# Regrouping VectorE's four steps of a unit, and TensorE's fills, in a four-layer selective scan

## The reference

```
delta = softplus(dt_proj(x) + bias)
h[t]  = exp(delta[t] * A[d, n]) * h[t-1] + (delta[t] * u[t]) * B[t, n]
y[t]  = sum over n of h[t][n] * C[t, n]  +  D * u[t]
```

## Time and profile before

| what | value |
|---|---|
| median of 3 runs | 36,397.4 us (36,394.3 to 36,398.0) |
| span of the profiled execution | 36,378.3 us |
| VectorE busy | 33,161.5 us, 91% |
| GpSimd busy | 30,847.6 us, 85% |
| TensorE busy | 26,866.7 us, 74% |
| ScalarE busy | 18,959.8 us, 52% |
| mean granted TensorE clock | 0.848 of full |
| multiplies of VectorE (L1051) | 6,240 |
| scans of VectorE in V units, in P units | 6,240 and 3,744 |

### The profile page before, as it was taken

The page is one execution under the profiler, slowest core; times in us unless marked ns, Lnnn a source line. Parts: engine busy times, 40 slices in busy tenths (PEclk is TensorE's granted clock), DMA queues, the critical chain, the costliest instruction groups (busy, mean ns, idle before and its releaser), DMA issues. The chain is left out here.

```text
span 36378.3 us, 340417 instructions
## 1 busy us (share of the span) xinstructions
PE 26866.7 (74%) x79280; PEld 8195.4 (23%) x79280; DVE 33161.5 (91%) x18001; ACT 18959.8 (52%) x23286; POOL 30847.6 (85%) x7804
## 2 busy tenths in 40 slices
PE   5777777777766777777777766777777777766777
PEld 2222222222222222222222222222222222222224
DVE  5999999999977999999999977999999999976993
ACT  4555555555534555555555534555555555534551
POOL 1999999999961999999999951999999999964994
PEclk7888888888888888888888888888888888887886
DMA  4666666666675666666666665666666666675665
GB/s 154 173 172 174 175 173 175 174 173 174 173 221 168 175 172 174 175 174 175 174 174 174 174 216 168 174 174 173 173 175 175 174 174 174 174 218 181 175 174 148
DMA packets 2423694, 6402.41 MB, mean 176 GB/s; under 512 B 703824, under 2 KB 875728, under 8 KB 2411728
## 3 DMA queue, kind: packets, MB, share of 16 engines
q1 hardware_dynamic: 2421968, 6387.69, 65.8%
HBM read 2986.75 MB, written 764.47 MB: 103 GB/s over the span
## 5 line engine op out<-in xcount | busy, mean ns | idle before, releaser
L1277 POOL TENSOR_TENSOR h<-h,c 128x2048 f32<-128x2048 f32 x4992 | 20780.7, 4179 | 660.1 <-DVE h L1077 522.6
L1077 DVE TENSOR_TENSOR_SCAN h<-decay,state,slot 128x1024 f32<-128x1024 f32 x6240 | 14647.7, 2347 | 789.0 <-ACT state L1221 32.3
L906 PE MATMUL slot<-bc,pick 96*128 96x512 bf16 x12496 | 4544.6, 452 | 7554.3 <-DVE h L1073 6883.1
L983 PE MATMUL psy<-h,t_fold 128*32 128x512 f32 x40000 | 9979.5, 671 | 0.0
L1073 DVE TENSOR_TENSOR_SCAN h<-slot,state,made 128x1024 f32<-128x1024 f32 x3744 | 8548.9, 2325 | 6.5 <-ACT slot L1116 5.3
L1298 POOL TENSOR_TENSOR made<-du,b 128x2048 f32<-128x2048 f32 x1872 | 7811.8, 4173 | 683.0 <-DMA b<-bcdram 683.0
L1116 ACT ACTIVATE decay<-delta,na 128x1024 f32<-128x1024 f32 x6248 | 7102.1, 1146 | 1892.8 <-DVE h L1077 1701.4
L1051 DVE TENSOR_TENSOR slot<-du,slot 128x1024 f32<-128x1024 f32 x6240 | 7540.3, 1208 | 374.1 <-PE slot L906 342.9
L1116 ACT ACTIVATE slot<-delta,na 128x1024 f32<-128x1024 f32 x3744 | 4181.7, 1117 | 4061.1 <-DVE h L1077 4046.9
L906 PEld LDWEIGHTS slot<-bc,pick 96*128 96x128 bf16 x12496 | 841.0, 103 | 12915.3 <-DVE h L1073 9747.3
L983 PEld LDWEIGHTS psy<-h,t_fold 128*32 128x32 f32 x40000 | 2098.1, 119 | 7316.1 <-issue 7055.7
(11 more groups left out here) (111 smaller groups left out, 19571.9 us busy)
## 6 DMA issues: line engine op xcount, KB each, us to landing
delta<-delta SPq DMA_DIRECT2D x10048, 128.0 KB, 2.5
du<-du SPq DMA_DIRECT2D x10048, 128.0 KB, 2.9
b<-bcdram SPq DMA_DIRECT2D x7520, 128.0 KB, 2.8
c<-bcdram SPq DMA_DIRECT2D x6720, 128.0 KB, 2.9
u<-useq SPq DMA_DIRECT2D x212, 1536.0 KB, 6.7
yseq<-ybuf SPq DMA_DIRECT2D x624, 512.0 KB, 2.8
ya<-yseq SPq DMA_DIRECT2D x420, 512.0 KB, 4.8
yb<-yseq SPq DMA_DIRECT2D x360, 512.0 KB, 5.8
```

The costliest lines, as they stand in the source:

```text
L906: mm = pe.matmul(slot[s % 2][:, cols], pick[:, rows_of, :], bc[q % 2][:, cols], start=True, stop=True)
L983: mm = pe.matmul(psy[rows, cols], T["fold"][:, :], h[v % H_RING][:, c, cols], start=(v % QUADS == 0), stop=(v % QUADS == QUADS - 1), skip_ ...
L1077: dve.tensor_tensor_scan(out, decay[s % DECAY_RING][:, order], slot[s % 2][:, order], first, ALU.mult, ALU.add).then_inc(sem["h_ready"], 1)
L1277: pool.tensor_tensor(both[:, :, 0:CH], both[:, :, 1:], c4[g][:, order].unsqueeze(1).broadcast_to((P, 2, CH)), ALU.mult)\
```

## The change

It does two things to the order inside the scan stage; no instruction is added or dropped.

- VectorE: within a V unit the order was multiply A, scan A, multiply B, scan B. It becomes multiply A, multiply B, scan A, scan B. P units keep scan A, scan B.
- TensorE: the fill of step s + 2 stood in every step s. Now both fills of a unit stand in the odd step, one behind the other, ahead of the step's other work. The halves of the four sums move from steps 4, 4, 5, 5, 6, 6, 7, 7 to 5, 5, 6, 6, 7, 7, 8, 8 (`SUM_AT`), and ScalarE's copy of delta from step 8 to step 9 (`TAKE_AT`).

```diff
-PARTS_AT, EXP_AT, LOG_AT, CORRECTION_AT, TAKE_AT = 2, 3, 4, 5, 8
-SUM_AT = (4, 4, 5, 5, 6, 6, 7, 7)
+PARTS_AT, EXP_AT, LOG_AT, CORRECTION_AT, TAKE_AT = 2, 3, 4, 5, 9
+SUM_AT = (5, 5, 6, 6, 7, 7, 8, 8)
...
                     for s in range(BS):
-                        fill_b(C0, s + FILL_LAG)
+                        if s % 2 == 1:
+                            fill_b(C0, s - 1 + FILL_LAG)
+                            fill_b(C0, s + FILL_LAG)
...
-                        for s in range(BS):
-                            q, t, n = place(s)
-                            if s // 2 not in on_pool:
-                                multiply(C0, body, s)
-                            scan(C0, body, s, g)
+                        for v in range(BU):
+                            if v not in on_pool:
+                                multiply(C0, body, 2 * v)
+                                multiply(C0, body, 2 * v + 1)
+                            scan(C0, body, 2 * v, g)
+                            scan(C0, body, 2 * v + 1, g)
```

## The result

The changed kernel takes 37,379.1 us (median of 4 runs, 37,370.0 to 37,382.5) against 36,397.7 for the kernel before beside it: ratio 1.027, 95% interval 1.0258 to 1.0283. It is 981 us slower. The forecast was slower by 502.

The account below looks back on a forecast made before the run. VectorE was taken as the bound, GpSimd nearly level. Terms summed to +0.80 us per tile, times 624 = +499, giving 36,900 us, 1.4% slower; own range 36,600 to 37,250, 8-in-10 range 36,150 to 37,480.

Parts of the forecast that it names:

- GpSimd's chain: Rival, chance 0.12: du's late start makes unit 7 late, B rows make unit 2 late; another 0.9 per tile, 37,460 us.
- VectorE's order: VectorE, V units: no instruction needs its direct predecessor, saving 1.95 us per tile (bounds 0 and 2.2).
- the late start isn't from the dependency: Rival on VectorE, chance 0.04: the 1.95 saving doesn't come, +1,217 on the forecast, 38,110 us.
- Multiply B behind a P unit: Units 0, 3, 6: multiply B waits 0.09 for TensorE's fill B, three times a tile; 0.25 us (bounds 0 and 0.3).
- Unit 1: TensorE's fill A late for unit 1, behind skip term, reduce and projection; 0.8 us per tile (bounds 0.2 and 1.6).
- the slow case: Unit 1 with fill B to next fill A taking 6.64 us: sum 8.48, so VectorE waits 1.62.
- Unit 4: TensorE late for unit 4, relu now behind fill B, mostly at the lower clock; 2.0 us per tile (bounds 0.5 and 2.8).
- Delta later: Delta out about 0.1 after unit 4, GpSimd's du some 2.3 later; 0.1 us per tile (bounds 0 and 1.0).
- Waits that go: VectorE's earlier waits for TensorE, 0.55 us per tile, of which 0.4 inside tiles was counted as saved.
- GpSimd's share: Sign: GpSimd's busy share in a scan window falls to about 0.95; a rise to 0.98 would refute the forecast.
- The wait for L906: Sign: the multiply's wait for TensorE's fill grows from 342.9 us to some 1,700 to 2,000, longest at unit 4.
- TensorE keeps up: Rival, chance 0.19: TensorE in time for units 1 and 4, GpSimd becomes the bound; 48.4 per tile, 35,590 us.

Follow-up runs that it names:

- e4: Changed kernel plus useless matmuls: relu term summed twice more in step 4, once more between unit 3's fills; 37,082.7 us, ratio 1.0192.
- e7: Changed kernel with SyncE's five loads of the next chunk moved ahead of its wait for GpSimd's gate of unit 2; 37,329.4 us, ratio 1.0258.
- e8: Changed kernel with the moves of e6 and e7 together; 35,734.2 us, ratio 0.9821 to the kernel before.
- e11: e8 with both halves of delta's projection in step 1, ahead of reduce; 35,745.1 us, ratio 0.9821 to the kernel before.
- e6: Changed kernel with sums ordered relu, ex, log, excess at steps 4,4,4,4,5,5,7,7 and delta copied at step 8; 36,553.3 us, ratio 1.0045.
- e14: e4 with the next chunk's loads ahead as in e7; 36,126.0 us, ratio 0.9924 to the kernel before.

## Why the prediction came out as it did

The direction and the mechanism were right; the size was half of what was measured (+502 against +981). The time lies inside the wide range, close to its upper end, but above the forecast's own range of 36,600 to 37,250. The wide range ends just above the price of GpSimd's chain (37,460), and that chain didn't happen: VectorE doesn't wait before unit 2 or unit 7. That the number is inside is in part luck.

- *VectorE's order*, 1.95 per tile: measured 5 x 0.40 = 2.0 (6.76 per V unit). The rival in which the late start isn't from the dependency is out: the pair of multiplies takes 2.27 from its start to scan A, 1.13 each, against 1.31 where the scan needs the multiply right before it. The Trainium skill's page VectorE: DVE Perf Modes (section The DRAIN you can't avoid) has it from a chain of copies that the semaphore costs nothing extra; that didn't carry over to these shapes.
- *Multiply B behind a P unit*, 0.25: about 0.1, of which 0.08 in unit 3, where the fill is nearly always slow, and 0.04 or less in each of the others.
- *Unit 1*, 0.8: 0.98. More skip matmuls were slow than before (86% against 59%), but the slow case was priced too high, at 1.62: in the tile shown reduce took 1.91 and not 2.32, and the wait was 1.10.
- *Unit 4*, 2.0: 2.53. This is the mis-sized term. The text argued that nearly every tile would meet the lower clock and worked out 2.37 for it, then took 2.0, with weight on cases that its own argument excluded. The relu matmuls (mean 1057 ns, 99% slow) show that there was hardly a fast case, and e4 that the whole wait was the clock's.
- *Delta later*, 0.1: GpSimd did wait for it, 3871.8 us in all instead of 2359.5, and at 51 us per tile VectorE didn't wait for GpSimd before unit 7. But SyncE issues the next chunk's loads behind its wait for GpSimd's gate, and they came too late for unit 6's fills, 0.24 per tile (e7). No term stood for this. The earlier trace rows had B rows that GpSimd waited for; the loads issued behind them weren't followed to TensorE.
- *Waits that go*, 0.4: the excess over the floor before was 0.36 per tile.

Together -2.0 + 0.1 + 0.98 + 2.53 + 0.24 - 0.36, and 0.07 before unit 0, are +1.56, times 624 = 973; the spans differ by 990. Against the forecast's +0.80 that is 0.76 more: 0.53 from unit 4 and 0.24 from unit 6, while the other differences nearly cancel.

Of the signs, the pitch of 1.12 to 1.14 and the rise of the relu matmuls came as named, and GpSimd's share fell to 0.93, a little further than 0.95. The wait for L906 went past its 1,700 to 2,000, to 2,490.

Of the rivals, "TensorE keeps up" was a real kernel, just not this one: its floor of 48.4 us per tile at GpSimd's 47.8 of work is what e8 and e11 reached, 48.6.

## What to carry to other kernels

Putting a consumer's independent instructions side by side pays only if the producer's deadline is worked out anew: here each fill had 3.6 us to be made before and 1.1 (fill B) or 2.3 us (fill A) after, and the work moved behind it ran at half the clock because the engine had idled just before. Use idle time ahead of a deadline, not the time behind the release, for work that has its inputs; and when one wait is removed, look first at the queue that is paced by the slowest engine, since e4 gave back seven tenths of what it won at unit 4, and e6 more than half, to loads that had been just in time.

## What was not expected of the hardware

Useless matmuls made the kernel faster. The same window in e7 and, with them added, in e14:

```profile
5000.00:6000.00 1000.00, 758.86 (x2209) 210.77 (x2209) 927.49 (x508) 537.98 (x673) 935.35 (x236) 0.85 0.66 168
5000.00:6000.00 1000.00, 850.24 (x2557) 251.88 (x2559) 969.80 (x533) 558.64 (x699) 976.85 (x246) 0.92 0.69 177
```

With three more relu terms per tile TensorE was busy 850 of 1000 us instead of 759, the granted clock rose from 0.85 to 0.92 in the same window, and the kernel went from 37,329 (e7) to 36,126 us (e14). What such work costs in power or on a chip with more cores at work wasn't tried.
